# q's residues and the wide reciprocals of the later small-head stages on GpSimd, their first part projected inside the MLP in front

## The reference, cut to what matters

```python
# block 2: 16 heads of 16; self attention, then cross attention on the context, then an MLP of 1024
scores = einsum('bhqd,bhkd->bhqk', q, k) / sqrt(16)
scores = scores * mask - 10000.0 * (1.0 - mask)
probs  = softmax(scores); out = einsum('bhqk,bhkd->bhqd', probs, v)
x = x + merge_heads(out) @ w_ao + b_ao          # twice, with a layernorm in front of each
x = x + gelu(layernorm(x) @ w1 + b1) @ w2 + b2
# block 3: 32 query heads of 8 over 8 key heads, cross attention, layernorm of the sum at the end
scores = einsum('bkgld,bksd->bkgls', q, k) / sqrt(8) + encoder_attention_mask
```

## Time and profile before

| | |
|---|---|
| time, median of 3 runs | 1602.65 us (1600.52 to 1605.79) |
| the profiled execution's own time | 1607.07 us |
| its span in the trace | 1605.0 us |
| PE, DVE, ACT, POOL busy over the span | 93%, 59%, 57%, 5% |
| mean granted TensorE clock | 0.981 |

### The profile page before, as it was taken

One profiled execution on the slowest core, in us unless ns is written; L12 is line 12 of the kernel. 1 busy time (PEld: TensorE's weight loads), 2 busy tenths in 40 slices (PEclk: granted clock), 3 DMA queues, 4 the chain that ended last, 5 costly groups with the idle time before them and its releaser, 6 DMA issues.

```text
span 1605.0 us, 28634 instructions
## 1 busy us (share of the span) xinstructions
PE 1493.2 (93%) x9824; PEld 1146.4 (71%) x9824; DVE 949.4 (59%) x3398; ACT 908.1 (57%) x2803; POOL 85.3 (5%) x89
## 2 busy tenths in 40 slices
PE   7999999999999999999999999997888879888886
PEld 5666687788787777778787878775656557755554
DVE  4777624545454455544455455238999991278885
ACT  5788824444444344444344444327888884388896
POOL 2000010000000001000000000110010010100000
PEclk9999999999999999999999999998999999999998
DMA  7000103010100101001010000010001000000000
GB/s 283 2 2 2 62 1 118 1 47 15 47 15 1 61 1 60 1 1 60 1 61 1 1 0 1 1 53 1 2 1 41 8 8 7 0 2 8 21 2 14
DMA packets 10878, 40.64 MB, mean 25 GB/s; under 512 B 2416, under 2 KB 2672, under 8 KB 8688
## 3 DMA queue, kind: packets, MB, share of 16 engines
q1 hardware_dynamic: 10736, 38.82, 6.8%
HBM read 37.77 MB, written 1.05 MB: 24 GB/s over the span
## 4 chain that ended last, share of the span: by engine, by line
PE 68%; DVE 11%; ACT 6%; issue 5%; DVEq 0%; POOLq 0%; POOL 0%; ACTq 0%
PE bank L726 7%; PE bank L707 7%; PE bank L740 7%; PE bank L699 7%; PE bank L686 7%; PE bank L689 7%; PE bank L666 5%; PE bank L655 5%; PE bank L715 4%; PE bank L545 3%; DVE probs L1121 3%; ACT probs L888 3%; DVE probs L1103 3%; PE bank L532 3%; DVE q_res L1067 2%
## 5 line engine op out<-in xcount | busy, mean ns | idle before, releaser
L888 ACT ACTIVATE probs<-probs,negmax 128x256 f32<-128x256 f32 (+1 forms) x640 | 346.9, 549 | 78.3 <-DVE negmax L1121 77.9
L959 ACT ACTIVATE pT<-bank 128x512 f32<-128x512 f32 x128 | 76.5, 597 | 387.8 <-PE bank L715 387.8
L545 PEld LDWEIGHTS bank<-ident,probs 128*128 128x128 f32 x1536 | 175.5, 145 | 110.6 <-issue 55.1
L545 PE MATMUL bank<-ident,probs 128*128 128x128 f32 x1536 | 232.4, 287 | 23.1 <-DVE pT L1129 12.5
L1236 DVE TENSOR_REDUCE stats<-bank 128x1 f32<-128x257 f32 x256 | 108.4, 425 | 212.4 <-PE bank L707 211.4
L1121 DVE CUSTOM_DVE_ANT_0 probs<-bank,mask_a 128x256 f32<-128x256 f32 (+1 forms) x384 | 176.2, 508 | 37.6 <-PE bank L532 33.4
L896 ACT ACTIVATE pT<-bank 128x512 f32<-128x512 f32 x304 | 178.1, 587 | 33.1 <-PE bank L545 32.9
L726 PE MATMUL bank<-pT,probs 128*128 128x256 f32 x512 | 132.6, 381 | 2.7 <-ACT pT L959 2.7
L707 PE MATMUL bank<-kT,pT 128*128 128x257 f32 x512 | 132.7, 382 | 0.6 <-ACT pT L942 0.6
L532 PE MATMUL bank<-kT,q_res 32*128 32x256 f32 (+1 forms) x1280 | 114.8, 465 | 17.0 <-DVE negmax L1121 13.8
L888 ACT ACTIVATION_READ_ACCUMULATOR probs<-probs,negmax 128x1 f32 x640 | 126.1, 197 | 0.0
(11 more groups left out here) (107 smaller groups left out, 2445.1 us busy)
## 6 DMA issues: line engine op xcount, KB each, us to landing
w_m<-in_w SPq DMA_DIRECT2D x6, 1024.0 KB, 7.1
g_qkv<-in_g SPq DMA_DIRECT2D x4, 1536.0 KB, 7.3
q_res<-in_g SPq DMA_DIRECT2D x4, 1536.0 KB, 6.3
w_qkv<-in_w SPq DMA_DIRECT2D x3, 768.0 KB, 4.3
g_bv<-in_gbv SPq DMA_DIRECT2D x8, 256.0 KB, 6.7
g_o<-in_go SPq DMA_DIRECT2D x4, 512.0 KB, 3.4
q_res<-in_go SPq DMA_DIRECT2D x4, 512.0 KB, 3.4
rows<-in_rows SPq DMA_DIRECT2D x1, 1664.0 KB, 14.0
```

Of the source, the lines that this page charges most:

```text
L545: last = nc.tensor.transpose(out[:, n * P:(n + 1) * P], probs[:, u % PROBS, q * T + t * P:q * T + (t + 1) * P], ident[:, :])
L888: last = nc.scalar.activation(s, s, ACT.Exp, bias=negmax[:, u % PROBS, k:k + 1], scale=-1.0, accum_out=sums[:, tile % 2, q, j * c.res + r: ...
```

## The change

1. In a2 and a3, q of every part but the first is taken from PSUM by ACT (two `Identity` activations with bias, into `q_all`, a view of the first g_qkv buffer), and POOL makes the residues from it in SBUF (new `residues`, with semaphore `a_spread`). The first part's q stays on DVE.
2. In a2 and a3, POOL spreads the reciprocals (new `widen`); DVE keeps the reciprocal itself.
3. q, k and v of the first part of a2 and a3 are projected by PE inside the last batch of the MLP in front, taken from PSUM by DVE and ACT there, and the first quad of scores is issued before the MLP's last product. The banks for them become 6, 7, 6.
4. The host's last rows are normalised by DVE at slot 3 and turned by PE at slot 10 instead of slot 0. In a2's first quad DVE alternates `times_mask` and `maxima`.
5. In a3 `vector_copies` goes from (0, 3, 6) to (0, 2, 4, 6): half of the copies on DVE.
6. POOL's list for the two stages is written by slots, to hold the new work.

```diff
-        got = [-1] if slot == 0 and self.host else []
+        got = [-1] if slot == 10 and self.host else []
-        return [7, 6, 4, 5, 7][m] if m < len(self.loads()) else 7
+        return ([6, 7, 6] if self.host else [7, 6, 4, 5, 7])[m] if m < len(self.loads()) else 7
+    def by_scalar(self, what, p):
+        return what[0] == "k" or self.spread(what, p)
+    def spread(self, what, p):
+        return what == "q" and p >= 1 and self.host is not None
-          scale=8.0 ** -0.5, vector_copies=(0, 3, 6), host="l3t"),
+          scale=8.0 ** -0.5, vector_copies=(0, 2, 4, 6), host="l3t"),
...
# PE, slot(): what the first quad of a part waits for
+                            if c.spread("q", p):
+                                pe.wait_ge(sem("a_spread"), st.at("a_spread", 0, p))
# PE, mlp(), in front of step f of the last batch
+                            if b == B - 1 and project:
+                                k = S["a2" if n == 1 else "a3"]
+                                pe.wait_ge(sem("a_kout"), k.at("a_kout", 0, 1))
                             turn_rows(own, b - 1, bank[7])
+                        if b == B - 1 and project:
+                            if f == 1:
...
+                                project("q", 0, 0)
+                            elif f == 2:
+                                project("q", 0, 1)
+                            elif f == 3:
+                                rows_turned(pe, own, b - 2)
+                                project("k0", 0, 0)
+                            elif f == 4:
+                                project("k0", 0, 1)
+                            elif f == 7:
+                                project("v0", 0, 0)
+                            elif f == 8:
+                                project("v0", 0, 1)
+                            elif f == 9:
+                                pe.wait_ge(sem("m_gelu"), st.at("m_gelu", b, FT))
+                                following(0)
...
# ACT
+                    if what == "q":
+                        for i in range(KT):
+                            last = nc.scalar.activation(q_all[:, p % 2, i, :], src[:, i * T:(i + 1) * T], ACT.Identity,
+                                                        bias=col(c.parts[p].qcol, i))
...
+                        if b == B - 1 and f == NORM_AT - 1 and keys:
+                            keys("k0", 0)
# DVE
+                    if c.host and tile >= 1:
+                        dve.wait_ge(sem("a_recip"), st.at("a_recip", 0, tile))
                     v.reciprocal(recip[:, :, 0:n], sums[:, tile % 2, :, 0:n]).then_inc(sem("a_inv"), 1)
+                    if c.host:
+                        return
...
                 if c.kinds == "mult":
-                    for u in range(QUAD):
-                        times_mask(u)
+                    times_mask(0)
...
+                        if c.kinds == "mult" and slot < 3:
+                            times_mask(slot + 1)
...
+                    if slot == 3 and c.host:
+                        norm_rows(c.host, B - 1, x_rows)
...
+                    if b == B - 1 and queries:
+                        queries(0)
+                        values("v0", 0)
                     added(dve, f"m{n}", b)
# POOL
+                def residues(p):
+                    m = c.evacuated("q", p)[1]
+                    pool.wait_ge(sem("a_kout"), st.at("a_kout", 0, m))
...
+                    for r in range(c.res):
+                        last = nc.gpsimd.tensor_scalar(to[:, :, r, :], q_all[:, p % 2, :, :], marks[c.res][:, r:r + 1],
+                                                       None, ALU.mult)
+                    last.then_inc(sem("a_spread"), 1)
+                def widen(tile):
+                    n = 4 * c.res
+                    pool.wait_ge(sem("a_inv"), st.at("a_inv", 0, tile + 1))
...
+                    for q in range(QT):
+                        last = nc.gpsimd.tensor_copy(recips[:, tile % 2, q, :].rearrange("p (n d) -> p n d", d=c.dh),
+                                                     recip[:, q, 0:n].rearrange("p (n o) -> p n o", o=1)
+                                                     .to_broadcast([P, n, c.dh]))
+                    last.then_inc(sem("a_recip"), 1)
```

More of the change, by code:

```diff
@@ L319, in small_stage @@
                 a_maskin0=0 if c.name == "0" else 32, a_maskin1=0 if c.name == "0" else 32, a_mask=5 if c.name == "2" else B,
-                a_proj=len(uses), a_kout=sum(w[0] == "k" for w in uses), a_pout=sum(w[0] != "k" for w in uses), a_scores=units,
+                a_proj=len(uses), a_kout=sum(w != "n" and c.by_scalar(w, p) for w, p in c.uses),
+                a_pout=sum(w != "n" and not c.by_scalar(w, p) for w, p in c.uses), a_scores=units,
+                a_spread=len(c.parts) - 1 if c.host else 0,
                 a_masked=units if c.kinds == "mult" else 0, a_max=units, a_exp=units, a_t=units,
@@ L620, in slot, with mlp @@
                             project(what, p, n)
-                for what in c.loads():
-                    project(what, 0, 0)
-                    project(what, 0, 1)
-                return slot
-            def mlp(n, before, own, after=None, c=None):
+                if c.name == "0":
+                    for what in c.loads():
+                        project(what, 0, 0)
+                        project(what, 0, 1)
+                return slot, project
+            def mlp(n, before, own, after=None, c=None, following=None, project=None):
                 st = S[f"m{n}"]
@@ L829, in _ @@
             pe.wait_ge(sem("d_tout"), end("b12", "d_tout"))
[L830 removed]
             pe.wait_ge(sem("s_w1"), 32)
+            c = SMALL[1]
+            slot, project = attention(c)
+            mlp(1, "l1m", "l21", following=slot, project=project)
             rows_turned(pe, "l21", B - 2)
[L833 to L837 removed]
+            for s in range(1, c.count + 2):
                 slot(s)
[L839 removed]
+            last, after = c, slot
             pe.wait_ge(sem("s_w1"), 64)
+            c = SMALL[2]
+            slot, project = attention(c)
+            mlp(2, "l23", "l3t", after, last, slot, project)
             rows_turned(pe, "l3t", B - 2)
[L842 to L846 removed]
+            for s in range(1, c.last_slot() + 1):
                 slot(s)
@@ L911, in attention, with mlp @@
                     for what, p in c.projected(ahead) if ahead >= 0 else []:
-                        if what[0] == "k":
+                        if c.by_scalar(what, p):
                             keys(what, p)
-            def mlp(n, gelu, before, own):
+            def mlp(n, gelu, before, own, keys=None):
                 st = S[f"m{n}"]
@@ L1196, in attention @@
                         for what, p in c.projected(s):
-                            if c.after(s + 1) == slot and what == "q":
+                            if c.after(s + 1) == slot and what == "q" and not c.spread(what, p):
                                 queries(p)
@@ L1200, in attention, with mlp @@
                                 values(what, p)
-            def mlp(n, before, own):
+            def mlp(n, before, own, queries=None, values=None):
                 st = S[f"m{n}"]
@@ new lines, in after2 @@
+            def after2(slot):
+                c = SMALL[1]
+                if slot == 12:
+                    pool.wait_ge(sem("l_z"), S["l21"].at("l_z", 0, B))
+                    bias("o2s", B - 1)
+                    additive(c, "2c", 0)
+                for b, x in enumerate([4 * c.units, 5 * c.units, 6 * c.units]):
+                    if slot == x + 5:
+                        additive(c, "2c", b + 1)
+                for b, x in enumerate([7 * c.units, 8 * c.units]):
+                    if slot == x + 5:
+                        additive(SMALL[2], "3", b)
+                for p, x in enumerate(c.parts):
+                    if slot == c.after(c.y_slot(p) + 1):
+                        power(x.norm, x.b)
+                    if slot == c.after(c.y_slot(p) + 1) + 3:
+                        pool.wait_ge(sem("l_z"), S[x.norm].at("l_z", 0, x.b + 1))
+                        bias("o2c" if x.norm == "l22" else "m2", x.b)
@@ L1385, in _, with after3 @@
+            def after3(slot):
+                c = SMALL[2]
+                if slot == 12:
+                    pool.wait_ge(sem("l_t"), S["l3t"].at("l_t", 0, B))
+                    bias("o3", B - 1)
+                for b in (2, 3):
+                    if slot == (b - 1) * c.units + 5:
+                        additive(c, "3", b)
+                for p, x in enumerate(c.parts):
+                    if slot == c.after(c.y_slot(p) + 1):
+                        power(x.norm, x.b)
             additive(SMALL[1], "2", 0)
-            for b in range(B):
+            for b in range(B - 1):
```

117 lines of the change are left out of this document (61 added, 56 removed).

## The result

The changed kernel takes 1595.08 us, median of 8 runs (1591.98 to 1598.03), against 1602.37 for the kernel before (8 runs, 1600.52 to 1605.79): ratio 0.9956, 95% interval 0.9945 to 0.9966. That is 7.3 us less, where 18.65 were forecast; it is faster by more than 0.3%, and inside the range (1571 to 1596), near its upper end.

The account below looks back on a forecast made before the run. DVE was taken to set a2's pace, with no engine full in a3. Terms -2.4 - 4.9 - 11.35 = -18.65 us, off the median 1602.65, gave 1584 us, range 1571 to 1596.

Parts of the forecast that it names:

- The starts: First parts of a2 and a3, projected inside the MLP in front: -2.4 us in a2, -7.75 in a3.
- The joint: From a2's last sum to a3's fifth unit; forecast as a3's start, fifth unit at 1401.8 against 1409.54: -7.75 us.
- a2, the other q: Parts 2 to 7 of a2: DVE saves 1.81 us each, loses 1.0 beside POOL; net -0.8 x 6 = -4.9 us.
- DVE sets the pace: Part of a2, DVE busy 29.89 of 31.58 us: a saved microsecond of DVE counts nearly fully.
- the granted clock: No term for it in a2's later parts; 0.5 us was added in a2's start, at 0.90.
- Rival A: a2 gives only its start, DVE blocked for all of POOL's added work or ACT late: 1588 us, chance 0.18.
- The wide reciprocals: a2, 14 tiles: DVE saves 0.28 us each, loses about 0.3 beside POOL's 0.25 copy: 0 us (-3.9 to +10).
- a3, pace: a3 behind its start: +0.8 over seven quads, -3.4 on q's quad, -2.6 over 32 units, +1.6 over the last 15 quads.
- seven quads, 5.18 each: a3 before the change, 1409.54 to 1445.81: the old quad length, against which the new quad was put at 5.29 us.
- nothing covers the 1.22 any more: a3's quads: no copy behind the last unit, so the 1.22 us for the next scores adds fully; quad 5.29 us.
- Rival B: a3: copies tie DVE to ACT, 16 more waiting 0.39 us for PE's turns, +6.2: 1590 us, chance 0.12.
- GpSimd's residue: POOL's residue instruction over 512 columns in a2 and a3: 0.62 us alone, 0.85 measured in a2.

Follow-up runs that it names:

- start_only: Kernel before with only the new start of a2 and a3; q, wide reciprocals on DVE and copies as before: 1597.93 us, ratio 0.9972.
- q_a3_only: Changed kernel with q's residues back on DVE in a2 alone: 1596.73 us, ratio 0.997 to the kernel before.
- c_odd: Changed kernel with a3's DVE copies at (1, 3, 5, 7) instead of (0, 2, 4, 6): 1585.24 us, ratio 0.9903 to the kernel before.
- odd_v12: c_odd with a2's projection of v begun one slot earlier (12 rather than 13): 1571.15 us, ratio 0.9812 to the kernel before.
- v12_q_dve: odd_v12 with a2's q residues back on DVE: 1580.78 us, ratio 0.9869 to the kernel before.
- turn_later: Changed kernel with the turn of the finished rows two slots later in a2 alone: 1616.27 us, ratio 1.0086 to the kernel before.
- odd_two_ops: c_odd with GpSimd's residue instruction given its second step (plus 0.0): 1584.26 us, ratio 0.9896 to the kernel before.
- best: odd_v12 with GpSimd's residue instruction given its second step: 1569.14 us, ratio 0.9801 to the kernel before.

## Why the prediction was too large

**The starts: right for a3, not for a2.** m1's last batch ran from 1056.95 to 1078.33, 21.38 us against 14.25 before (1059.36 to 1073.61): +7.1 for +7.0, and PE stood 0.48 us in front of the turn for my 0.65. The fifth unit of a2 came 1.35 us earlier against the third sum, for 2.4: PE idled 6.4 us behind the first scores, where I had 5. The joint gave 8.1 for 7.75. The labels were off in both: start_only puts 2.3 of the joint's gain down to the q of a3's second part, and all of a2's 1.35 down to q (35.49 us with the new start alone, 35.42 before). In a2 what the projections gained by lying in the MLP just paid for the 7.1 us that they cost there.

**a2, the other q: the step that failed first.** The sum had -4.9; the rest of a2 gave 1.7, and q_a3_only says 1.6 for the whole move, its start included. The price was not what failed. I had 1.8 saved less 1.0 taken back beside GpSimd; the trace has some 0.75 taken back, so 1.05 a part was there to be had. Two steps failed. The first is "DVE sets the pace", read from 29.89 busy of 31.58: PE's wait of 3.1 us for v, with ACT behind it, is in the kernel before as well, and with it in place 1.33 us less work on DVE shorten a part by 0.57 at one clock. The second is a term that I put at nothing, the granted clock: I left it as it was, and it came out lower in more parts than in q_a3_only, at 0.87 us each. The part of the earlier trace rows, my measure, was itself one with the lower clock (0.89); parts with 1.00 took 30.6 already before. Besides, the last stretch of a2, where no q was made before either, became 1.8 longer (28.34 to 30.14, clock 0.99 to 0.89; in c_odd it is 29.69 at 0.99). Rival A, in which a2 gives only its start, came near in its result, but not for its reasons: neither was VectorE blocked for all of GpSimd's work nor did ScalarE become late. odd_v12 (-14 us) and v12_q_dve (+9.6) show that the wait held a2: with it gone, q's move is worth 0.2 to 1.2 us in five parts at full clock, 0.95 on average, where 0.8 was forecast.

**The wide reciprocals: right at 0.** A copy is 0.36 us for my 0.25, and taking them back changed nothing that a comparison can tell.

**a3, pace: the third step that failed.** The quad of the new kind is as I worked it out (5.29 forecast, 5.26 in the trace, with the 1.22 uncovered), and so is that q's quads get shorter: 8.72 became 5.78. Mis-sized was the term it was compared with: "seven quads, 5.18 each" included the first of them, 6.16 long, right behind q. The plain ones took 4.98, so the copies' places cost 0.28 on each of some 17 quads, 4.8 us, and about 3 more in the quads with outputs (7.11, 7.97, 7.09 where 7.0, 6.43, 6.8 stood). With 5.8 saved on the two q quads (6.8 by my sum) that makes +2.0 for the forecast -3.6; the trace has +2.1. In two other traces of the same a3 (turn_later, q_a3_only) it is +0.2 and +0.5, so the miss is 4 to 6 us. I had the mechanism in the text ("nothing covers the 1.22 any more") and priced it at 0.11 a quad, some +3.3 over 30 quads, where it came to about 8; c_odd undoes just that and gives 10 us. Rival B looked for the loss at the other end, VectorE waiting for PE's turns: that is 7.5 us in all of a3, and 13.0 in c_odd, which is faster.

**GpSimd's residue: wrong by 2.5 times, without effect.** 1.56 us against 0.62, from a row of the same width but with two steps. odd_two_ops and best show that it didn't matter. The Trainium skill's rule ("SBUF — State Buffer", section "Who interferes with whom"), that such instructions exclude each other, holds in part: beside 3.40 us of residues DVE lost 0.75.

**Sum.** Forecast -2.4, -4.9, 0, -7.75, -3.6. By the traces -1.35, -1.7, (within a2), -8.1, +2.1: together -9.0, and -7.3 in the medians. That the time still lies within the stated range is because the range was wide enough for two such misses; the sum itself was too large by 11 us.

## What to carry to other kernels

An engine that is busy 95% of a loop need not set its pace alone: look for the one instruction of another engine that waits on it (here 3.11 us for a bank), and move that producer a slot earlier, before taking work off the engine. Compare loops at one granted clock, and look at several of them: one part of a2 alone was not typical. Work that an engine must do for another can be put where it waits for that other anyway: a quad with two copies took 5.26 us with both in front of its last unit and 4.65 with one of them behind it. When a new period is compared with an old one, take both from quads of the same kind; a mean over seven that holds one odd quad ate the sign of this term.

## What was not expected of the hardware

GpSimd's multiply of 128x512 float32 in its one-step form takes 1.56 us (1.49 with a constant), and 0.69 to 0.77 with a second step that adds 0.0. The granted clock fell behind one wait of PE of 3.1 us, but not behind each: the four turns after it took 1.11 us (lower level) in five of six parts of the changed kernel and in two of six of q_a3_only, and 0.66 (upper level) in the others. With that wait at 0.5 us (odd_v12) they took 0.66 in all six, and the clock was 1.00 over each stretch but the first (0.94). What tells the parts with the same wait apart stays open.
